# Normalising the attention heads half by half instead of step by step

## The reference, cut to what matters

```python
attn = softmax(einsum('bhqd,bhkd->bhqk', qh, kh) * SCALE)     # 16 heads, 16 wide
out = einsum('bhqk,bhkd->bhqd', attn, vh)
out = out.transpose(0, 2, 1, 3).reshape(B, SQ, DIM)
return out @ Wo.T + bo
```

## Time and profile before

| | |
|---|---|
| Median of 3 runs | 3608.37 us (3608.07 to 3608.52) |
| Profiled execution | 3603.33 us, of which its span is 3601.5 us |
| TensorE's granted clock, mean | 0.989 of full speed |
| PE busy | 3488.3 us, 97% of the span |
| DVE busy | 2764.0 us, 77% |
| POOL busy | 2507.6 us, 70% |
| ACT busy | 1715.7 us, 48% |

### The profile page before, as it was taken

The page is one execution under the profiler, slowest core; times in us unless marked ns, Lnnn a source line. Parts: engine busy times, 40 slices in busy tenths (PEclk is TensorE's granted clock), DMA queues, the critical chain, the costliest instruction groups (busy, mean ns, idle before and its releaser), DMA issues.

```text
span 3601.5 us, 97036 instructions
## 1 busy us (share of the span) xinstructions
PE 3488.3 (97%) x38789; PEld 2853.8 (79%) x38789; DVE 2764.0 (77%) x6256; ACT 1715.7 (48%) x4049; POOL 2507.6 (70%) x3159
## 2 busy tenths in 40 slices
PE   6699999999999999999999999999999999999998
PEld 5578888888888888888888888888888888888876
DVE  5677787787787787787787877877877877877863
ACT  2345545545545445445545545445445455455443
POOL 5767777777777677677677777777677677677742
PEclk8899999999999999999999999999999999999999
DMA  5111111111121121121121121111111111111100
GB/s 177 48 50 59 61 67 53 66 69 48 67 72 45 67 74 45 67 74 45 67 74 45 67 73 46 67 67 53 67 63 57 67 60 60 67 57 62 67 8 10
DMA packets 87098, 221.54 MB, mean 62 GB/s; under 512 B 8262, under 2 KB 53634, under 8 KB 70274
## 3 DMA queue, kind: packets, MB, share of 16 engines
q1 hardware_dynamic: 86658, 215.34, 16.9%
HBM read 164.92 MB, written 50.39 MB: 60 GB/s over the span
## 4 chain that ended last, share of the span: by engine, by line
PE 93%; DVE 4%; ACT 2%; issue 1%; POOL 0%; DMA 0%; SPq 0%; DVEq 0%; ACTq 0%
PE ps L869 13%; PE ps L860 13%; PE ps L722 11%; PE ps L700 10%; PE ps L839 9%; PE ps L756 8%; PE ps L811 8%; PE ps L788 6%; PE ps L728 5%; PE ps L680 3%; PE ps L780 3%; PE ps L849 2%; DVE held L1355 1%; PE ps L750 1%; ACT rest L1002 1%; DVE nmax_pair L1292 1%
## 5 line engine op out<-in xcount | busy, mean ns | idle before, releaser
L1124 POOL TENSOR_TENSOR chunks<-v_windows,xT 128x560 f32<-128x560 f32 (+1 forms) x384 | 870.8, 2284 | 259.0 <-DVE xT L1267 155.0
L1292 DVE TENSOR_REDUCE nmax_pair<-ps 128x4 f32<-128x480 f32 (+2 forms) x1280 | 776.1, 669 | 167.8 <-PE ps L756 167.5
L1119 POOL TENSOR_TENSOR chunks<-rest,k_windows 128x512 f32<-128x512 f32 (+1 forms) x384 | 552.9, 1455 | 436.8 <-DVE xT L1246 232.6
L969 ACT ACTIVATE prob<-ps 128x256 f32<-128x256 f32 (+2 forms) x1536 | 670.0, 548 | 331.9 <-PE ps L788 331.9
L860 PE MATMUL ps<-xT,w_up 128*128 128x256 f32 x2048 | 483.7, 384 | 0.0
L869 PE MATMUL ps<-w_down,held 128*128 128x256 f32 x2048 | 458.9, 382 | 1.8 <-DVE held L1355 1.6
L869 PEld LDWEIGHTS ps<-w_down,held 128*128 128x128 f32 x2048 | 383.9, 190 | 72.2 <-issue 20.4
L860 PEld LDWEIGHTS ps<-xT,w_up 128*128 128x128 f32 x2048 | 375.7, 191 | 44.7 <-issue 0.9
L1246 DVE TENSOR_REDUCE xT<-chunks 128x32 f32<-128x512 f32 (+1 forms) x384 | 294.0, 766 | 128.0 <-POOL chunks L1119 128.0
L927 ACT COPY xT<-ps 128x512 f32<-128x512 f32 x256 | 149.8, 585 | 489.3 <-PE ps L680 489.2
L1136 POOL TENSOR_SCALAR_AFFINE_SELECT prob<-prob 128x512 f32<-128x512 f32 x512 | 319.5, 655 | 75.7 <-ACT prob L969 75.7
(11 more groups left out here) (146 smaller groups left out, 6086.6 us busy)
## 6 DMA issues: line engine op xcount, KB each, us to landing
k_windows<-passed_on SPq DMA_DIRECT2D x64, 1024.0 KB, 4.6
v_windows<-passed_on SPq DMA_DIRECT2D x64, 1024.0 KB, 5.1
x<-in_x SPq DMA_DIRECT2D x64, 256.0 KB, 2.9
passed_on<-rest SPq DMA_DIRECT2D x64, 256.0 KB, 2.0
passed_on<-held SPq DMA_DIRECT2D x64, 256.0 KB, 2.0
out<-x SPq DMA_DIRECT2D x64, 256.0 KB, 2.1
y<-in_ctx SPq DMA_DIRECT2D x64, 120.0 KB, 2.8
w_up<-in_up SPq DMA_DIRECT2D x1, 1024.0 KB, 8.8
```

The costliest lines, as they stand in the source:

```text
L969: last = nc.scalar.activation(prob_pair(seq, L, m)[0:keys, :, r, col:col + qs], of_pair, ACT.Exp, scale=SCALE)
L1119: last = nc.gpsimd.tensor_tensor(chunk_of(c).rearrange("p (j d) -> p j d", d=D), q_row, window("k", (b + first) * D, (D, n), (1, D)), ALU. ...
L1124: last = nc.gpsimd.tensor_tensor(chunk_of(c).rearrange("p (h i j) -> p h i j", i=HD, j=WINDOW), window("v", b * D + first * HD, (HD, n), ( ...
L1292: nc.vector.tensor_reduce(nmax[s][:, tb, heads], src, AX_X, ALU.max, negate=True).then_inc(emptied[b], 1)
```

## The change

`normalise` becomes one loop over the two halves with all four steps inside. No instruction is added or removed, none changes its shape, and the other engines' lists stay as they are. What changes is the order of eight DVE instructions and what each of them waits for.

```diff
-                        for m in range(2):
-                            halves.append(bank("values", seq, (L, m)))
-                            in_bank = ps[:, halves[m], :]
-                            nc.vector.transpose(in_bank, in_bank).then_inc(dve_step, 1)
...
-                        steps[0] += 4
-                        for m in range(2):
-                            dve.wait_ge(dve_step, steps[0] - 3 + m)
-                            nc.vector.reciprocal(sums[m], shares[m][:, :, :, HD]).then_inc(dve_step, 1)
-                        for m in range(2):
-                            dve.wait_ge(dve_step, steps[0] - 1 + m)
+                            half_bank = bank("values", seq, (L, m))
+                            in_bank = ps[:, half_bank, :]
+                            settle(nc.vector.transpose(in_bank, in_bank))
+
+                            shares = in_bank.rearrange("p (e j i) -> p e j i", e=2, i=SLOT)
+                            sums = rsum[s][:, m, :].rearrange("p (e j) -> p e j", e=2)
+                            settle(nc.vector.reciprocal(sums, shares[:, :, :, HD]))
                             nc.vector.tensor_tensor(o[s][:, m, :].rearrange("p (j e i) -> p e j i", e=2, i=HD),
...
+                                                    ALU.mult).then_inc(emptied[half_bank], 1)
-                        for m in range(2):
                             wait_taken(dve, "values", seq, L, m)
                             last = nc.vector.transpose(xT[s][:, m, :], o[s][:, m, :])
                         last.then_inc(attended[s], 1)
```

More of the change, by code:

```diff
@@ L1308, in _ @@
                         L, = args
-                        halves, sums, shares = [], [], []
                         for m in range(2):
-                            halves.append(bank("values", seq, (L, m)))
-                            in_bank = ps[:, halves[m], :]
-                            nc.vector.transpose(in_bank, in_bank).then_inc(dve_step, 1)
-                            shares.append(in_bank.rearrange("p (e j i) -> p e j i", e=2, i=SLOT))
-                            sums.append(rsum[s][:, m, :].rearrange("p (e j) -> p e j", e=2))
-                        steps[0] += 4
-                        for m in range(2):
-                            dve.wait_ge(dve_step, steps[0] - 3 + m)
-                            nc.vector.reciprocal(sums[m], shares[m][:, :, :, HD]).then_inc(dve_step, 1)
-                        for m in range(2):
-                            dve.wait_ge(dve_step, steps[0] - 1 + m)
+                            half_bank = bank("values", seq, (L, m))
[4 more added lines that the diff above has]
+                            settle(nc.vector.reciprocal(sums, shares[:, :, :, HD]))
                             nc.vector.tensor_tensor(o[s][:, m, :].rearrange("p (j e i) -> p e j i", e=2, i=HD),
-                                                    shares[m][:, :, :, 0:HD],
-                                                    sums[m].unsqueeze(3).to_broadcast([P, 2, T // 32, HD]),
-                                                    ALU.mult).then_inc(emptied[halves[m]], 1)
-                        for m in range(2):
+                                                    shares[:, :, :, 0:HD],
+                                                    sums.unsqueeze(3).to_broadcast([P, 2, T // 32, HD]),
+                                                    ALU.mult).then_inc(emptied[half_bank], 1)
                             wait_taken(dve, "values", seq, L, m)
```

## The result

| | before | changed |
|---|---|---|
| Median | 3608.22 us (3600.97 to 3608.52, 4 runs) | 3680.16 us (3677.02 to 3685.18, 4 runs) |
| Ratio | | 1.0204, 95% interval 1.0192 to 1.0216 |
| Profiled execution | 3603.33 us | 3682.75 us, span 3681.0 us |

72 us more, where I had forecast 44 and a range up to 3672. The direction and the place of the loss were right; its size was not.

A forecast was written before the change was run, and what follows sets the result against it. PE was taken to bound the kernel, with `normalise` results just in time; 0.71 us lateness beyond the covers costs 0.43 + 0.31 = 0.74 us a sequence, 59 x 0.74 = 44, so 3608.4 + 44 = 3652 us, range 3630 to 3672.

The forecast's parts named there:

- What bounds the kernel: PE, busy 97% of the span; DVE at 77% has room only on average, its results reaching PE just in time.
- distances of 0.23 and 0.35 us: From the end of `normalise`'s last turn to PE's first `project_out` load: 0.23 us cross layer, 0.35 us causal.
- covers of 0.28 and 0.40: Lateness of `normalise` in us that costs PE nothing at `project_out`: 0.28 in the cross layer, 0.40 in the causal.
- DVE does not catch up and each layer pays anew: Each `normalise` starts with DVE's distance to PE restored, so delays add up: 0.43 and 0.31 us, 0.74 a sequence.
- The lateness, 0.71 us: How much later DVE finishes `normalise` at `attended`: 3.62 us from first start to last end instead of 2.91.
- The five other sequences, at nothing: Sequences at start and end, outside the 59 steady ones, assumed to add nothing; PE and DVE wait for each other there.
- The range: 3630 to 3672 us for the changed kernel, taking in nearly all of the forecast's bounds.
- Free waits: Rival: waiting on DVE's own last instruction costs nothing, so order inside `normalise` is indifferent; 3608 us, chance 0.05.
- Half 0 going ahead under PE: Rival: DVE works off half 0 while PE fills half 1; faster, 3604 us at best, chance 0.02.
- The second stall: Rival: PE also waits at L750 for the bank freed by the add into `y`; about 3679 us, chance 0.08.
- its condition, a lateness above 0.82: At L750, lateness beyond 0.70 us DVE can lose plus 0.12 spare is paid again, 6 us per tenth.
- Signs in the profile: `normalise` about 3.6 us, PE waiting before L839, more idle on PEld than PE, sequence about 55.1 us, PE busy nearly unchanged.

The follow-up runs named there:

- the split signal: The changed kernel, but each turn raises `attended` and `project_out` waits for half 1 only before its second matmul: 3634.49 us, ratio 1.0070.
- the cover given back on both engines: The changed kernel with PE's cross `project_out` behind the next projection and DVE's evacuation of cross v behind the causal `normalise`: 3631.42 us, ratio 1.0065.

## Why the prediction was right in kind and wrong in size

- **What bounds the kernel; distances of 0.23 and 0.35 us; covers of 0.28 and 0.40.** Right. Four kernels in which `normalise` got 0.54 to 0.88 us longer follow (lateness - 0.28) + (lateness - 0.40), or one of the terms alone: 0.40, 1.04, 1.08 and 0.48 by the formula; 0.40, 1.03, 1.07 and 0.47 measured. Those with 0.26 and 0.28 paid nothing in the steady part. The formula does not reach further: it was low for the split signal (0.41 against 0.22) and for the cover given back on both engines (0.26 against 0.15), and it says nothing of the kernels with the causal `normalise` ahead of the reduction.
- **DVE does not catch up and each layer pays anew.** Right: waits in both layers of nearly every sequence, 114 in the steady part.
- **The lateness, 0.71 us.** This is the step that failed, in its size: it measured 0.88. The 0.034 us of idle time per handover was right. Wrong were the lengths that I put beside it: the mean lengths of the reciprocal, product and turn in the trace of before (0.230, 0.396, 0.419), in which each of them overlaps a neighbour. Where they wait for the one in front they last 0.257, 0.424 and 0.445. Six of those (each of the three, in both halves) make 6 x 0.027 = 0.16, nearly all of the difference. Why they last longer is not shown. 59 x 2 x 0.17 = 20 us of the 28 that were missing.
- **The five other sequences, at nothing.** Mis-sized too. Between the medians, 72 - 63 = 9 us are outside the steady pattern. In the profiled execution they are 15: 2.7 at the start, 12.4 at the end, of which 9.7 are PE's own busy time at a lower clock. All kernels here had 1 to 9 us of this sort beyond 59 times their sequence. I did not settle how much of it is the change. A part of the end's 12.4 comes without any loss in the steady part: the kernel with product and turn by halves, whose sequence is that of before, shows 5.0 us more of PE's busy time in its end (168.60 against 163.63) at a granted clock of 0.95, and its end is 6.0 us longer:

```profile
3416.45:3607.60 191.15, 168.60 (x1802) 135.29 (x1800) 99.37 (x237) 75.12 (x189) 64.50 (x111) 0.95 0.03 8
```

- **The range.** It went to 3672, by a lateness of 0.87, which is what was measured; but with nothing for the edges it ended below the median.
- **Rivals.** Free waits: refuted by the run with the old order and six waits. Half 0 going ahead under PE: no trace of it, DVE's waits at the bank transposes fell from 2.4 to 1.3 us, and the one large wait for L1317 grew from 1.9 to 3.0. The second stall: not in the changed kernel, although its condition, a lateness above 0.82, was met by 0.88. The condition was worked out wrongly: it set PE's own delay at 0.31, while with 0.88 PE comes 0.48 later, so that DVE has 0.39 + 0.48 + 0.12 = 0.99 to lose. Here DVE is done with the reduction at 1024.63, still 0.12 ahead of the add, and L750's load comes 0.22 behind the add, where it was 0.18:

```profile
1022.72 1.99 PE L839 MATMUL ps<-w_causal_o,xT 128*128 128x256 f32 x8 [0.21 <-DVE xT L1322]
...
1023.91 0.72 DVE L1246 TENSOR_REDUCE held<-chunks 128x80 f32<-128x560 f32 x1
...
1024.75 0.69 DVE L1332 TENSOR_TENSOR y<-y,ps 128x512 f32<-128x512 f32 x1
...
1025.66 0.27 PEld L750 LDWEIGHTS ps<-mask_rows,pick_rows 32*128 32x128 bf16 x16
```

- **Signs in the profile.** PE's idle time was forecast as much smaller than the loss, and it is: 30.6 us in that row within the steady part, against a loss of 64, since PE's modelled end of the matmul in front covers a part. PE's busy time was forecast as nearly the same; it grew by 44.7 us, 32.6 of them in the steady part, with the same matmuls.

## What to carry to other kernels

Interleaving two independent chains on an engine hid each handover here; ordering them chain by chain exposed every one, 0.88 us in eight instructions with none added. Whether that matters is decided by the distance between the result and its reader, read from the timeline and not from busy shares: here 0.28 us of lateness were free, and beyond 0.40 every tenth of a microsecond cost 12 us. And before moving an instruction out of the way, look at who waits for it: the reduction that went behind a 3.8 us `normalise` cost more than the stall that it cured.

## What the runs showed of the hardware beyond what I expected

A DVE instruction that waits for the one in front not only starts 0.034 us behind its end; it also lasts 0.027 us longer than the mean of its kind in the order of the kernel before (reciprocal 128x16: 257 against 230 ns; product 128x256: 424 against 396; transpose 128x256: 445 against 419). A product that did not wait for the one in front measured 374 to 396 by the order around it. From a product's start to that of the next instruction it was 0.31 us (two products and their followers in 0.63) and is now 0.46. `project_out` with its first load late by x cost x - 0.11 us (after a late load its matmuls end 1.99 us behind the load, in the flow 2.10), but held up between its second and third load it cost the full delay (0.42 us of late loads, 0.41 measured). And the granted clock of the last 200 us differed between executions (0.98, 0.95 and 0.92 in the three shown), and PE's busy time there was 5.0 and 9.7 us longer at the two lower ones, for the same matmuls.
